# Opening of a one-core transformer kernel: folds moved into the first network's first block, VectorE normalising blocks 4 to 7

## The reference, cut to what matters

```
x: 4 x 1024 tokens of 128 numbers (4096 tokens)
x = x + 0.5 * L0_ffn(layernorm(x))      # the stage beside which the change lies
x = x + L0_attn(layernorm(x))           # its weights are folded ahead of time
x = x + 0.5 * L0_ffn(layernorm(x))
x = x + 0.5 * L1_ffn(layernorm(x))
x = x + L1_attn(layernorm(x))
x = x + 0.5 * L1_ffn(layernorm(x))

L0_ffn(x): gates = sigmoid(x @ expert_sel.T)          # 32 experts
           keep the 4 largest gates of a token, 0 elsewhere
           scores = relu(x @ keys) * gates            # 32 experts x 64 = 2048 hidden
           out = scores @ values
```

## Time and profile before

| | us |
|---|---|
| median of 3 runs | 1649.67 |
| lowest, highest | 1648.46, 1650.84 |
| the profiled execution, its own time | 1646.87 |
| its span in the trace | 1645.1 |
| PE turns block 6, block 7 of the opening | 36.67, 39.52 |
| first up product of the first network starts | 50.53 |
| first down product starts | 56.63 |
| second block of the network starts (its gates are spread) | 68.96 |

### The profile page before, as it was taken

How to read it: one execution, slowest core, us unless ns; L and a number is a source line. 1 busy time by engine, 2 the same in 40 slices (tenths; PEclk the granted TensorE clock), 3 DMA queues, 4 the chain that set the end, 5 groups by cost and what they waited for, 6 DMA issues and landing times.

```text
span 1645.1 us, 28122 instructions
## 1 busy us (share of the span) xinstructions
PE 1442.1 (88%) x8269; PEld 1095.3 (67%) x8269; DVE 1345.3 (82%) x3897; ACT 1026.5 (62%) x2300; POOL 856.8 (52%) x745
## 2 busy tenths in 40 slices
PE   5999998997999995999639999999999899779991
PEld 4777877654666663999527666666666666459880
DVE  7599998666667776888779999999999867768887
ACT  7544442365323233889668999999999723259880
POOL 5856662210133334467646666666666215537772
PEclk9999998999999997999869999999999999879995
DMA  9992001000011103222199900000000001122225
GB/s 196 179 177 34 1 6 48 1 1 1 26 33 33 45 19 89 60 74 74 49 212 181 163 1 1 2 1 1 1 1 2 1 14 36 43 56 74 72 59 153
DMA packets 156499, 91.24 MB, mean 55 GB/s; under 512 B 19414, under 2 KB 151207, under 8 KB 156353
## 3 DMA queue, kind: packets, MB, share of 16 engines
q1 hardware_dynamic: 142464, 70.52, 22.3%
q0 software_dynamic: 9664, 16.89, 3.2%
q10 hardware_dynamic: 4224, 2.10, 0.4%
HBM read 31.93 MB, written 60.53 MB: 56 GB/s over the span
## 4 chain that ended last, share of the span: by engine, by line
PE 55%; issue 12%; DVE 12%; POOL 10%; ACT 8%; DMA 2%; POOLq 0%; SPq 0%; DVEq 0%; ACTq 0%
PE psum L1379 9%; POOL answers L2443 8%; PE psum L2829 8%; PE psum L2854 5%; PE psum L661 5%; PE psum L662 4%; PE psum L663 4%; ACT psum L2935 4%; DVE psum L2955 3%; PE psum L2807 2%; PE psum L2808 2%; PE psum L2809 2%; PE psum L1134 1%; PE psum L1136 1%; PE psum L1135 1%
## 5 line engine op out<-in xcount | busy, mean ns | idle before, releaser
L2935 ACT ACTIVATE psum<-psum,gate 128x128 f32<-128x128 f32 (+7 forms) x512 | 368.6, 729 | 33.2 <-DVE gate L2955 31.5
L2955 DVE CUSTOM_DVE_ANT_0 psum<-psum,cmask 128x128 f32<-128x128 f32 (+7 forms) x512 | 371.0, 791 | 12.7 <-PE psum L2829 11.4
L1379 PE MATMUL psum<-raw_all,w 128*128 128x512 f32 x384 | 195.4, 592 | 1.5 <-DVE raw_all L1522 1.5
L661 PE MATMUL psum<-xl,wreg 128*128 128x512 f32 x320 | 181.6, 567 | 2.8 <-ACT psum L2935 1.5
L1520 DVE SCALAR_TENSOR_TENSOR raw_all<-psum,hg 128x512 f32<-128x512 f32 x128 | 88.1, 690 | 57.3 <-PE psum L663 55.2
L662 PE MATMUL psum<-xh,wreg 128*128 128x512 f32 x320 | 126.9, 397 | 0.0
L663 PE MATMUL psum<-xh,wreg 128*128 128x512 f32 x320 | 126.7, 396 | 0.0
L2829 PE MATMUL psum<-hh,hl 64*128 64x384 f32 (+3 forms) x768 | 114.4, 373 | 12.7 <-ACT psum L2935 12.7
L2829 PE MATMUL psum<-spare_sets_room 64*128 64x384 f32 (+3 forms) x768 | 114.0, 369 | 12.3 <-ACT psum L2935 12.3
L2443 POOL DMA_INDIRECT answers<-ed,xl x90 | 99.9, 1109 | 31.1 <-issue 30.8
L2829 PEld LDWEIGHTS psum<-hh,hl 64*128 64x128 f32 x768 | 86.3, 190 | 40.7 <-ACT psum L2935 33.7
(11 more groups left out here) (440 smaller groups left out, 4220.9 us busy)
## 6 DMA issues: line engine op xcount, KB each, us to landing
rows<-blank SPq DMA_DIRECT2D x146, 258.0 KB, 6.7
xl<-rows SPq DMA_DIRECT2D x58, 193.5 KB
raw_all<-answers SPq DMA_DIRECT2D x32, 256.0 KB, 4.1
w<-in_L_ffn_W_dram SPq DMA_DIRECT2D x16, 256.0 KB
x<-in_L_attn_x_dram SPq DMA_DIRECT2D x4, 512.0 KB, 5.6
out_dram<-x ACTq DMA_DIRECT2D x8, 256.0 KB, 4.1
answers<-ed,xl POOLq DMA_INDIRECT x90
answers<-row,xl POOLq DMA_INDIRECT x84
```

The source lines that it names most:

```text
L661: pe.matmul(dst, wh, xl[:, blk(i)], start=start, stop=False)
L1379: pe.matmul(bank(B_OUT[i % 2]), col(dn, j), hidden[:, n % HID, :], start=(j == 0), stop=(j == nf - 1)).then_inc(S["dn_done"], 1)
L2935: return act.activation(src, src, ACT.Exp, bias=kept_at(arg, u, q, a), scale=-1.0, accum_out=kept_at(esum, u, q, a))
L2955: return dve.tensor_tensor_reduce(src, src, mask, 1.0, 3e38, ALU.add, ALU.min, kept_at(arg, u, q, a))
```

## The change

What it does, part by part:

- **Loads.** SP issues the 13 small loads ahead of the four of `rawD`.
- **Rounding.** ScalarE rounds the up weights one block sooner, behind the squash of block 0. The down weights and `w0` stay at the same places of its loop.
- **Normalise.** ScalarE normalises blocks 0 to 3 only. VectorE normalises blocks 4 to 7, each ahead of the `choose` of blocks 0 to 3, by a `tensor_scalar` for each tile.
- **GpSimd.** Ahead of the network it now takes `xl` of blocks 0 to 5, the four up quarters and two of the four down quarters. The last two `xl`, `w0` and the two fold rests stand inside the network's first block, behind steps 3, 5, 7, 9 and 11.
- **VectorE** takes the other two down quarters, ahead of the network.
- **Folds.** Their PE products stand behind the up products 0, 1, 2 and 4 of the first block, their copies behind ScalarE's `hh` of the same steps. They have a buffer of their own (`fold_room`), so the wait of `hh` for `raw_read` is gone.

The core of the diff:

```diff
@@ sync
-            values = I["L0_ffn_values"].rearrange("e (j k) d -> k e j d", j=NF0)
-            for k in range(P // E0):
-                sp.dma_start(rawD[k * E0:(k + 1) * E0], values[k]).then_inc(d_load, 16)
             sp.dma_start(rawG[:], I["L1_ffn_Wg"]).then_inc(w_load, 16)
...
+            values = I["L0_ffn_values"].rearrange("e (j k) d -> k e j d", j=NF0)
+            for k in range(P // E0):
+                sp.dma_start(rawD[k * E0:(k + 1) * E0], values[k]).then_inc(d_load, 16)
@@ gpsimd
+            for i in range(LOWS_FIRST):
+                low(pool, i)
+                if i >= 2:
+                    rest_of(pool, 0, i - 2, 4).then_inc(S["rest_done"], 1)
+            for part in range(2):
+                last = rest_of(pool, 1, part, 4)
+            last.then_inc(S["rest_done"], 1)
+
+        LOWS_FIRST = HALF + 2
...
+        def late_pool(pool, j):
+            if j in (3, 5):
+                low(pool, LOWS_FIRST + (j - 3) // 2)
+            if j == 7:
+                rest_of(pool, 2, 0, 1)
+            if j in (9, 11):
+                k = (j - 9) // 2
                 pool.wait_ge(fold_raw, k + 1)
                 pool.wait_ge(fold_out, k + 1)
+                w = (wkp, wqp)[k]
                 pool.tensor_tensor(w[:, 1], raw_fold[:, k, :], w[:, 0].bitcast(F32), ALU.subtract).then_inc(S["raw_read"], 1)
+
+        FOLD_AT = {0: 0, 1: 1, 2: 2, 4: 3}
@@ scalar
-                if i < NB:
+                if i < HALF:
                     normalise(i)
...
-                if i == 3:
+                if i == 2:
                     round_weights(0, u_load, 1)
...
-            for k in range(4):
-                fold(k)
@@ vector
+            def normalise(i):
+                dve.wait_ge(S["xT_done"], i - 1)
+                for t in range(BT):
+                    at = i * BT + t
+                    last = dve.tensor_scalar(ed[:, i % 2, t, :], x[:, at, :], aggr[:, at, 0:1], y_all[:, at:at + 1],
+                                             ALU.subtract, ALU.mult)
+                last.then_inc(S["xn_dve"], 1)
...
             for k in range(CHOSEN):
+                if k < NB - HALF:
+                    normalise(HALF + k)
                 choose(dve, k)
...
+            for part in range(2, 4):
+                last = rest_of(dve, 1, part, 4)
+            last.then_inc(S["rest_dve"], 1)
@@ gated: tensor
-                    pe.wait_ge(ahead["rest_done"], 2)
+                    pe.wait_ge(ahead["rest_done"], 4)
...
+                if n == nf // 2:
+                    pe.wait_ge(ahead["rest_dve"], 1)
+                if n == nf:
                     pe.wait_ge(ahead["folds_out"], 1)
```

More of the change, by code:

```diff
@@ L84 @@
     next: object
+@dataclass
+class Folds:
+    tensor: Callable
+    scalar: Callable
+    gpsimd: Callable
 @dataclass
@@ L450, in gpsimd @@
             pool.tensor_copy(iota[0:1, 0:1], iota[0:1, 0:1]).then_inc(consts, 1)
[L452 to L462, removed]
@@ new lines, in gpsimd, with low, rest_of @@
+            for part in range(2):
+                last = rest_of(pool, 1, part, 4)
+            last.then_inc(S["rest_done"], 1)
+        LOWS_FIRST = HALF + 2
+        def low(pool, i):
+            pool.wait_ge(S["xT_out"], i + 1)
+            pool.wait_ge(S["xh_done"], i + 1)
+            pool.tensor_tensor(xl[:, blk(i)], xT[:, blk(i)], xh[:, blk(i)].bitcast(F32), ALU.subtract).then_inc(S["xT_read"], 1)
+        def rest_of(e, k, part, parts):
+            hi, lo, w = weights[k]
+            e.wait_ge(cast, k + 1)
+            step = w.shape[1] // parts
+            some = slice(part * step, (part + 1) * step)
+            return e.tensor_tensor(lo[:, some], w[:, some], hi[:, some].bitcast(F32), ALU.subtract)
@@ new lines, in late_pe @@
+        def late_pe(pe, j):
+            if j not in FOLD_AT:
+                return
+            k = FOLD_AT[j]
+            if k < 2:
+                pe.wait_ge(wp_out, 3)
+                pe.matmul(bank((B_V, B_W)[k]), turned_w[:, k * P:(k + 1) * P], pbd, start=True, stop=True).then_inc(folded, 1)
+            elif k == 2:
+                pe.wait_ge(a_hi, 1)
+                pe.wait_ge(S["centred"], 1)
+                pe.matmul(bank(B_M), b_cols, pbd, start=True, stop=True).then_inc(folded, 1)
+            else:
+                pe.wait_ge(fold_out, 1)
+                for c in range(NCH):
+                    last = pe.matmul(bank(B_V)[:, c:c + 1], pbd[:, c * P:(c + 1) * P], bcol[:, 0:1], start=True, stop=True)
+                last.then_inc(folded, 1)
@@ L528, in tensor @@
                     small_ones()
-                if i >= 7:
-                    for k in range(2):
-                        fold(2 * (i - 7) + k)
         def scalar(act):
             def normalise(i):
-                act.wait_ge(S["set"], i // HALF + 1)
+                act.wait_ge(S["set"], 1)
                 wait_past(act, S["xT_done"], i - 1)
@@ L1254, in one_block @@
                         low(i, j, at == 0)
+                    if i == 0:
+                        folds.gpsimd(pool, j)
             all_blocks(pool, one_block)
@@ L3000, in program @@
     def program():
-        opening, choose_late = setup()
-        ffn_1, late = gated("f0", opening.S, choose_late, dn=(f_dnh, f_dnl), **ffn)
+        opening, choose_late, folds = setup()
+        ffn_1, late = gated("f0", opening.S, choose_late, folds, dn=(f_dnh, f_dnl), **ffn)
         keys, end_pe, end_dve = linear_kv(ffn_1.S, late)
```

87 lines of the change are left out of this document (39 added, 48 removed).

## The result

| | before | changed |
|---|---|---|
| median of 5 runs, us | 1648.46 | 1659.07 |
| lowest to highest | 1643.49 to 1650.84 | 1658.15 to 1664.75 |
| ratio, 95% interval | | 1.0074, 1.0053 to 1.0096 |
| span of the profiled execution | 1645.1 | 1657.7 |
| mean granted clock | 0.951 | 0.952 |

The change makes the kernel slower by 0.74%. The forecast was slower by 4.6 us, at 1654.3 with a range up to 1657.5; the measured difference is 10.6 us, and 1659.07 lies above the range.

The account below looks back on a forecast made before the run. Ahead of the network PE was taken as the bound, fed by ScalarE. Opening -0.3, folds +3.1 and GpSimd +1.8 summed to +4.6 us on 1649.67, so 1654.3 us, range 1647.5 to 1657.5.

Parts of the forecast that it names:

- Term A: Opening, up to the network's first up product: it comes at 50.2 against 50.5, -0.3 us.
- alternation: Opening: VectorE and GpSimd take turns at the port, so four `tensor_scalar` cost about 5 us with GpSimd busy.
- Rivals one: Opening: VectorE keeps the port for a block's four instructions; first up product at 47.9, sum +2.3, 1652.0 us; chance 0.18.
- two (a `tensor_scalar` hardly waits): Opening: only the choices wait for GpSimd; first gate 5.8 us sooner, sum -1.8, 1647.9 us; chance 0.12.
- three (free of GpSimd, first up product at 42.5): Opening: GpSimd's queue doesn't hold VectorE, ScalarE and PE bound it; sum -4.0, 1645.7 us; chance 0.07.
- Term B: Network's first block: fold products on PE, taken at the upper clock level, cost +3.1 us, ends +2.8 and +6.7.
- rival four: First block: PE stays at 1.2 GHz through the folds, ScalarE's 2.3 us lie bare; sum +8.2, 1657.9 us; chance 0.08.
- Term C: Network's first block: GpSimd's added work and VectorE's hold of the port cost +1.8 us, ends 0 and +3.
- Two of its covers: Opening: `rawD` lands 3 us before ScalarE wants it; choices, centring and quarters end 1.5 us before the first gate; no cost.
- The rest: Dropped and later waits give or cost nothing; from block 1 on the network only passes its delay on.
- The rule of turns: Between waiting VectorE and GpSimd, one VectorE instruction slips in after each GpSimd instruction, read from rows at 254.48.
- the 6.7 us that the turn is later: Opening: the last turn at 46.2 against 39.52, a delay said to eat what the folds' leaving gave.

Follow-up runs that it names:

- norm_scalar: The changed kernel with ScalarE normalising all eight blocks again; ratio to the kernel before 1.0050 (1.0031 to 1.0068).
- both_m2: The changed kernel with ScalarE normalising all blocks, folds back in the opening, VectorE's three memsets made one; ratio to the kernel before 1.0011 (0.9996 to 1.0026).
- lows_ahead: The changed kernel with ScalarE normalising all blocks, VectorE's three memsets made one, two `xl` and `w0` back in the opening; ratio to the kernel before 0.9991.
- null: The kernel before, unchanged, timed against itself; ratio 0.9992 (0.9979 to 1.0006).

## Why the prediction was wrong

**The opening held.** Term A: forecast -0.3 by alternation, measured 49.20 - 50.53 = -1.3; the four of block 5 took 5.43 us ("about 5"), turn 6 came at 41.82 (43 forecast), the last turn at 45.02 (46.2). Rivals one (the port kept by VectorE, 2.3 us for block 5), two (a `tensor_scalar` hardly waits) and three (free of GpSimd, first up product at 42.5) fell; what three wrongly got from VectorE, ScalarE delivers: 43.98 in `norm_scalar`. Term B: first up to first down product 57.99 - 49.20 = 8.79 against 6.10, +2.7, forecast +3.1; the clock rose during the first fold (up matmuls of 0.63 us at 50.20 and of 0.40 us at 52.91), and the next folds took 1.02 us where one took 2.06 before, so rival four fell. Term C: from there to the end 190.08 against 187.58 before, +2.5, forecast +1.8, and `both_m2` and `lows_ahead` show that it is GpSimd's. The sum is +3.9 for +4.6. Two of its covers held too: the loads, and the choices ahead of the first gate (52.42).

**The step that failed** is the last of "The rest": "From block 1 on all is relative to block 0, and the network passes its delay on", and with it the sum, which went from the network's end straight to the end of the program. The delay was passed on, but behind the network the program is not the same: VectorE's has 17 instructions more, its pauses, one block of 128 instructions apart, fall on other instructions, and at 618 one decides a race for the port: +2.9 us. No term, no rival and no part of the range allowed a change of the opening to cost something at 618. The rest, 3 to 4 us, I neither forecast nor explained. Opening, network and event alone (3.9 + 2.9 = 6.8 on 1648.46) would have given 1655.3, inside the range; the rest put the time above it, and its cause stays open: the step of the clock at 264 may be a part of it. The width failed with it: the range had 3.2 us above the forecast, and two profiles of the same kernel (before and `null`) differ by steps of this size.

**The rule of turns** was right where it was read and wrong as a rule. "one VectorE instruction slips in after each GpSimd instruction" fits 27.8 to 33.2. At 617.95 VectorE asked during an indirect DMA and got no turn until the two `tensor_tensor` behind it were done. The Trainium skill, SBUF — State Buffer, section "SBUF: two separate sides", has the lock for a whole instruction. By that, with a turn at the next change of instruction, the comparison would have started by 618.4 or 619.7; it ended at 621.1.

**The reading of the parts.** The sum was right and its headings hid the sign of the parts. I had the folds as a cost (B) against "the 6.7 us that the turn is later". In phase and at the network's end the fold move gains 3.0 to 3.7 us; VectorE's normalising loses 5.0 to 5.7, since ScalarE had been able to do it by 39.5; GpSimd's five instructions lose 2.3 to 2.6.

## What to carry to other kernels

Work moved to an idle engine that shares a port with a busy queue costs turns of that queue (here 5.43 and 4.23 us), not its own 1.1 us; look first whether the old engine was late at all. Fill an engine's gap (GpSimd's 12 us) before putting its work into a loop that runs at its limit. And when a small edit changes a long program's time far from the edit, count the instructions of each engine: a program longer by two in a place of no account cost 10 us here, and its twin with 128 more cost 3, so compare variants in the same phase, and look for places where a few tenths of a us decide which engine gets the shared port.

## What the runs showed of the hardware

- VectorE shows pauses of 0.2 to 0.35 us at places with the remainder 63 when its instructions are counted in 128s, waits included (21 in 19 profiles). Packets of 8192 bytes on the queue of kind "instruction" come at the same rate, one for each 128 instructions, and near these places. Most such places show no pause.
- A VectorE comparison of two arrays that starts 0.18 to 0.22 us behind a GpSimd indirect DMA with two `tensor_tensor` behind it runs in 0.30 us (85 cases); one that starts 0.48 to 0.55 us behind takes 3.1 us and ends when the two are done (10 cases). Where another DMA follows in their place, it runs in 0.30 us at 0.46 to 0.70 us too (16 cases).
- Of two profiles of the same kernel, one had PE's clock at its lower level for some 7 us behind the gap between two stages and the other had not, 2.9 us apart.
